# A graph network on one core: the 4-head attention layers carry segment maxima by VectorE transpositions, with fewer TensorE products and one GpSimd wait less

## The reference

```python
z = (x @ W).reshape(n, 4, 64)
el = jnp.sum(z * al, axis=-1)
er = jnp.sum(z * ar, axis=-1)
e = leaky_relu(el[src] + er[dst], 0.2)
e_max = segment_max(e, dst)
ex = jnp.exp(e - e_max[dst])
alpha = ex / segment_sum(ex, dst)[dst]
out = segment_sum(z[src] * alpha[:, :, None], dst) + x + b
out = elu(out)
```

## Time and profile before

| | |
|---|---|
| median of three timed runs | 3638.85 us |
| span of the profiled execution | 4213.3 us (the page gives no other time of it) |
| TensorE products / weight loads | 3393.7 us (81%) / 2079.6 us (49%) |
| VectorE | 1955.5 us (46%) |
| ScalarE | 1189.6 us (28%) |
| GpSimd | 1440.0 us (34%) |
| granted TensorE clock, mean | 0.787 of 2.4 GHz |
| 8-head layer | about 350 to 1260 us of the span |
| layers 1 to 4, by adjacency | about 1400 to 2560 us |
| 4-head layers | about 2580 to 3290 and 3370 to 4090 us |

### The profile page before, as it was taken

How to read it: one execution, slowest core, us unless ns; L and a number is a source line. 1 busy time by engine, 2 the same in 40 slices (tenths; PEclk the granted TensorE clock), 3 DMA queues, 4 the chain that set the end, 5 groups by cost and what they waited for, 6 DMA issues and landing times.

```text
span 4213.3 us, 58454 instructions
## 1 busy us (share of the span) xinstructions
PE 3393.7 (81%) x16476; PEld 2079.6 (49%) x16477; DVE 1955.5 (46%) x4442; ACT 1189.6 (28%) x3024; POOL 1440.0 (34%) x1472
## 2 busy tenths in 40 slices
PE   5887777777777999999999985777778757777766
PEld 3444554454554556456555553555555434555543
DVE  5986666666665200000024013444545734445556
ACT  2663333333331101001001004333333243333333
POOL 5003444444430302103003003655555255555530
PEclk8997887878786999999989997666666756566676
DMA  6235555555550231332311322333333133333320
GB/s 201 98 119 139 138 148 137 141 138 142 147 139 1 81 99 40 112 90 63 99 46 50 103 65 75 110 107 106 106 106 105 54 98 109 106 104 106 108 61 31
DMA packets 236395, 424.63 MB, mean 101 GB/s; under 512 B 51419, under 2 KB 152720, under 8 KB 235966
## 3 DMA queue, kind: packets, MB, share of 16 engines
q1 hardware_dynamic: 175549, 248.26, 20.3%
q0 software_dynamic: 60544, 173.03, 15.1%
HBM read 381.52 MB, written 39.62 MB: 100 GB/s over the span
## 4 chain that ended last, share of the span: by engine, by line
PE 54%; DVE 16%; issue 11%; another core or an unknown queue 10%; ACT 4%; DMA 2%; DVEq 2%; SPq 1%; ACTq 0%; POOL 0%; POOLq 0%
PE ps L734 20%; PE ps L807 9%; PE ps L612 3%; PE ps L577 3%; PE ps L968 3%; DVE norm L1438 2%; PE ps L948 2%; PE ps L918 2%; PE ps L910 2%; DVE rows L1569 1%; DVE inv L1675 1%; ACT norm L1117 1%; PE ps L801 1%; DVE spread L1428 1%
## 5 line engine op out<-in xcount | busy, mean ns | idle before, releaser
L2041 POOL DMA_INDIRECT rows<-table,src_idx x1248 | 1215.3, 974 | 1134.5 <-DVEq L1357 422.9
L734 PE MATMUL ps<-rows,rT 128*128 128x448 f16 (+1 forms) x3200 | 816.5, 342 | 16.8 <-DMA rows<-adjacency 16.8
L734 PE MATMUL ps<-rows,spread 128*128 128x448 f16 (+1 forms) x1600 | 546.5, 342 | 0.0
L734 PEld LDWEIGHTS ps<-rows,rT 128*128 128x128 bf16 x3200 | 311.9, 98 | 278.0 <-issue 25.0
L807 PE MATMUL ps<-rows,spread 128*128 128x260 f32 x832 | 364.2, 587 | 66.5 <-issue 59.4
L807 PE MATMUL ps<-rows,w_roots 128*128 128x260 f32 x832 | 359.0, 578 | 54.4 <-issue 52.2
L1454 DVE TENSOR_TENSOR rows<-ps,norm 128x896 f32<-128x896 f32 (+1 forms) x24 | 24.7, 1028 | 674.2 <-PE ps L734 674.2
L1995 POOL CAST rT<-rows 128x1024 bf16<-128x1024 f32 (+1 forms) x28 | 26.6, 950 | 868.9 <-ACT rows L1212 868.9
L577 PE MATMUL ps<-rT,spread 128*128 128x272 f32 x832 | 284.0, 471 | 36.8 <-DVE norm L1256 20.3
L612 PE MATMUL ps<-rows,rT 128*128 128x272 f32 x832 | 293.3, 511 | 2.5 <-DVE rows L1310 2.5
L807 PEld LDWEIGHTS ps<-rows,spread 128*128 128x128 f32 x832 | 225.7, 290 | 130.3 <-issue 84.6
(11 more groups left out here) (266 smaller groups left out, 5067.6 us busy)
## 6 DMA issues: line engine op xcount, KB each, us to landing
rows<-adjacency SPq DMA_DIRECT2D x140, 560.0 KB, 3.7
rT<-table SPq DMA_DIRECT2D x416, 136.0 KB
spread<-in_tiles SPq DMA_DIRECT2D x104, 256.0 KB
rows<-table,src_idx POOLq DMA_INDIRECT x1248
w_table<-in_tiles SPq DMA_DIRECT2D x52, 256.0 KB
adjacency<-rT SPq DMA_DIRECT2D x4, 2800.0 KB, 10.6
adjacency<-acc SPq DMA_DIRECT2D x3, 2800.0 KB, 11.7
table<-rows SPq DMA_DIRECT2D x12, 528.0 KB, 3.0
```

The lines of the kernel that those rows point to most:

```text
L734: ins = mm(chunk_ps[c % 2][:, f, 0:width], xp[k][:, t, f * P:(f + 1) * P], ring[c][q][:, i, :], start=t == 0 and k == 0, stop=t == ROWS - ...
L2041: pool.indirect_dma_start(src_rows(l, par)[:, k, :], None, tables[l][:, :], bass.IndirectOffsetOnAxis(ap=src_idx[:, g * T + k:g * T + k + ...
```

## The change

In the 4-head layers:
- `spread_scores` makes one product of 12 columns for each tile; the three parts stay apart in PSUM, and `edge_scores` first adds them by a VectorE reduction, ahead of its wait for the gathered rows.
- `edges` and `carries` of TensorE go. `carry` transposes the row ends of both scans (32x32) into `ends_row`, with the forward ends on partition 0 and the backward ends on partition 1, takes the maximum of the scans (before, the first operation of `maxima`), scans both ways over two partitions, copies the last value, and transposes two blocks back into a column (`carry_of`).
- `rescales` makes one product with `resc_by_f`, which ScalarE forms by a second exponential from the rescaling factor and a constant row that is 0 for the feature half of a head and very negative for the other.
- The two halves of the step's second sums are joined.
- SP loads the end penalties with one transfer instead of two; a group has three transfers.
- GpSimd no longer waits for `er_ready` at the fifth gather.
- VectorE's chained steps of one group are 8 instead of 5. The setup makes the new constants and no longer those of `perm`.

```diff
@@ gat_pe
-                    for part in range(PARTS):
-                        ins = mm(er_ps[:, k * H:(k + 1) * H], turned_hot[:, par, k, :],
-                                 near[:, par, k, part * H:(part + 1) * H], start=part == 0, stop=part == PARTS - 1)
+                    ins = mm(er_ps[:, k, :, :].rearrange("p k h -> p (k h)"), turned_hot[:, par, k, :], near[:, par, k, :],
+                             start=True, stop=True)
...
-                for f in range(FC):
-                    ins = mm(gat_resc_ps[:, f:f + 1], head_of[H][:, f, :], resc_h[par][0:H, :], start=True, stop=True)
-                ins.then_inc(resc_ready, 1)
+                mm(gat_resc_ps, head_any[:, :], resc_by_f[par][:, :], start=True, stop=True).then_inc(resc_ready, 1)
...
-                if n is not None:
-                    edges(n)
-                    if not is_last(n):
-                        spread_scores(n + 1, *next_group(j, h, 2))
-                sums(g, j, 1, range(4, 6))
-                if n is not None:
-                    carries(n)
-                sum_tiles(j % 2, j, range(6, 8)).then_inc(node_ready, 1)
+                if n is not None and not is_last(n):
+                    spread_scores(n + 1, *next_group(j, h, 2))
+                sums(g, j, 1, range(4, 8)).then_inc(node_ready, 1)
@@ gat_act, weights
+                nc.scalar.activation(resc_by_f[b % 2][:, :], other_f[:, :], ACT.Exp, bias=rescale[0:H, :])
@@ gat_dve
-                rows_landed(dve, l, b, h)
                 dve.wait_ge(er_ready, gl + n + 1)
-                ch.then(V.tensor_tensor(grid(al), er_ps.rearrange("p (t h) -> p t h", h=H), src_rows(l, b)[:, :, D:D + H], ALU.add))
+                ch.then(V.tensor_reduce(grid(al), er_ps.rearrange("p t k h -> p t h k"), AX.X, ALU.add))
+                rows_landed(dve, l, b, h)
+                ch.then(V.tensor_tensor(grid(al), grid(al), src_rows(l, b)[:, :, D:D + H], ALU.add))
...
+                dve.wait_ge(scans_ready, ag + n + 1)
+                ch.done(V.transpose(ends_row.rearrange("p h s -> p s h")[:, 1:T + 1, :], walks[0:TH, P - 1:P + 31]))
+                ch.then(V.tensor_tensor(gat_max_ps, fwd[0:TH, :], bwd[0:TH, :], ALU.max))
+                pr = gat_pen_row[:, j, :, :].rearrange("p h s -> p (h s)")
+                ends = ends_row[0:2, :, :].rearrange("p h s -> p (h s)")
+                V.tensor_tensor_scan(linked[0:2, 0:HL], pr, ends, -BIG, ALU.add, ALU.max)
+                ch.then(V.tensor_tensor_scan(linked[0:2, HL:2 * HL][:, ::-1], pr[:, ::-1], ends[:, ::-1], -BIG, ALU.add, ALU.max))
+                V.tensor_copy(ends_row[0:2, :, 0:1], linked[0:2, 0:HL].rearrange("p (h s) -> p h s", h=H)[:, :, T:T + 1])
+                into = linked[:, :].rearrange("p (j x) -> p j x", j=2)[:, :, 0:HL].rearrange("p j (h s) -> p j s h", h=H)
+                return ch.done(V.transpose(carry_of[:, :].rearrange("p (j t h) -> p j t h", j=2, h=H), into[:, :, 0:T, :]))
...
-                                                   carry_ps[0:TH, j:j + 1], gat_max_ps, ALU.add, ALU.max))
+                                                   carry_of[:, 33 * j:33 * j + 1], gat_max_ps, ALU.add, ALU.max))
@@ SP, seg
-                    for k in range(2):
-                        at = (2 * j + k) * H * SLOTS
-                        sp.dma_start(gat_pen_row[0:1, at:at + H * SLOTS].rearrange("o (h s) -> o h s", h=H)[:, :, 1 - k:SLOTS - k],
-                                     pen_ends[k:k + 1, bass.ds(g * T, T)].unsqueeze(1)
-                                     .broadcast_to([1, H, T])).then_inc(gat_seg_landed[j], 16)
+                    sp.dma_start(gat_pen_row[:, j, :, 1:T + 1],
+                                 pen_ends[:, bass.ds(g * T, T)].unsqueeze(1).broadcast_to([2, H, T])).then_inc(gat_seg_landed[j], 16)
@@ gpsimd
-                        if kind == "gat" and g > 0 and k == T // 2:
-                            wait_alone(pool, er_ready, NG * (l - 5) + g)
```

More of the change, by code:

```diff
@@ L53 @@
 SLOTS = T + 1
+LINKS = T + 2
 LAYERS = [("gat_edge", 8, D + 16), ("sum", 0, D), ("sum", 0, D), ("sum", 0, D), ("sum", 0, D),
@@ L73 @@
     STORES.append([v + _in_hbm * (b == _c % 2) for b, v in enumerate(STORES[-1])])
-SEG_LOADS = {0: 48, 5: 64, 6: 64}
+SEG_LOADS = {0: 48, 5: 48, 6: 48}
 SEGS = 4
@@ L181, in gnn_program @@
         left = sb("left", [P, 2, 4, 4])
-        gat_pen_row = sb("gat_pen_row", [1, SEGS * 2 * 4 * SLOTS])
+        gat_pen_row = sb("gat_pen_row", [2, SEGS, 4, LINKS])
         edge_pen_row = sb("edge_pen_row", [1, 4 * 8 * SLOTS])
-        perm = sb("perm", [33, 2, 4, SLOTS])
+        ends_row = sb("ends_row", [32, 4, LINKS])
+        linked = sb("linked", [32, 2 * (4 * LINKS + 2)])
+        carry_of = sb("carry_of", [32, 2 * 32])
         edge_perm = sb("edge_perm", [65, 2, 8, SLOTS])
@@ L238, in gnn_program @@
         resc_h = [sb(f"resc_h{p}", [8, 1]) for p in range(2)]
+        resc_by_f = [sb(f"resc_by_f{p}", [4, FC]) for p in range(2)]
+        head_any = sb("head_any", [4, P])
+        other_f = sb("other_f", [4, FC])
         part = [rows[:, i * FC * CW:(i + 1) * FC * CW].rearrange("p (f n) -> p f n", f=FC) for i in range(4)]
@@ L777, in turn_scores @@
                 nc.tensor.transpose(alT_ps[0:TH, :], al3[:, 0:TH], ident[:, :]).then_inc(alT_ready, 1)
[L779 to L790, removed]
             def turn_back(n):
@@ L867, in gat_pe @@
             turn_scores(0)
-            edges(0)
-            carries(0)
             turn_back(0)
@@ L1515, in gat_dve @@
             TH = T * H
-            HS = H * SLOTS
+            HL = H * LINKS
             ag, gl = NG * ATT.index(l), NG * (l - 5)
@@ L1541, in carry @@
             def carry(n, j):
[L1542 to L1548, removed]
@@ L1557, in maxima @@
+                V.tensor_copy(ends_row[0:2, :, 0:1], linked[0:2, 0:HL].rearrange("p (h s) -> p h s", h=H)[:, :, T:T + 1])
+                into = linked[:, :].rearrange("p (j x) -> p j x", j=2)[:, :, 0:HL].rearrange("p j (h s) -> p j s h", h=H)
+                return ch.done(V.transpose(carry_of[:, :].rearrange("p (j t h) -> p j t h", j=2, h=H), into[:, :, 0:T, :]))
+            def maxima(n, at, carried_at):
+                ch.wait(carried_at)
                 for j, into in ((0, gat_max_ps), (1, segmax[0:TH, :])):
@@ L1558, in maxima @@
                     ch.then(V.scalar_tensor_tensor(into, gat_pens[at][0:TH, P + 1 + j * P:2 * P + 1 + j * P],
-                                                   carry_ps[0:TH, j:j + 1], gat_max_ps, ALU.add, ALU.max))
+                                                   carry_of[:, 33 * j:33 * j + 1], gat_max_ps, ALU.add, ALU.max))
                 V.tensor_tensor(shifted[0:TH, :], alT_ps[0:TH, :], segmax[0:TH, :], ALU.subtract)
-                V.tensor_scalar(rescale[0:H, :], carry_ps[0:H, 0:1], segmax[0:H, 0:1], 0.0, ALU.subtract,
+                V.tensor_scalar(rescale[0:H, :], carry_of[0:H, 0:1], segmax[0:H, 0:1], 0.0, ALU.subtract,
@@ L1628, in step @@
                 if n is not None:
-                    carry(n, b)
+                    carried_at = carry(n, b)
                 rescale_node(g, j % 2)
                 if n is not None:
-                    maxima(n, b)
-            edge_row = perm[TH:TH + 1, :, :, :]
-            V.memset(fwd[TH:TH + 1, :], 1.0)
-            V.memset(bwd[TH:TH + 1, :], 1.0)
-            ch.then(V.memset(edge_row, 0.0))
-            ch.then(V.memset(edge_row[:, 0, :, 0:1], -BIG))
-            ch.then(V.memset(edge_row[:, 1, :, T:SLOTS], -BIG))
+                    maxima(n, b, carried_at)
+            V.memset(linked[:, :], 0.0)
+            ch.then(V.memset(ends_row[:, :, :], -BIG))
             turned_hots(0, 0, 0)
@@ L1642, in gat_dve @@
             scans(0, 0)
-            carry(0, 0)
-            maxima(0, 0)
+            maxima(0, 0, carry(0, 0))
             turned_hots(1, 1, 0)
@@ L2174, in _ @@
                 ins = V.tensor_tensor(ends_of_tile[:, j, :], seg_of_tile[:, :, x], seg_of_tile[:, :, y], ALU.not_equal)
-            V.memset(perm[:, :, :, :], 0.0)
+            V.tensor_tensor(head_any[:, :], head_of[4][:, 0, :], head_of[4][:, 1, :], ALU.add)
+            ch.then(V.tensor_tensor(other_f[:, :].unsqueeze(2), head_of[4][:, :, 0:1], head_of[4][:, :, P - 1:P], ALU.max))
             V.tensor_copy(ident16[:, :], ident[:, :])
-            V.memset(gat_pen_row[:, :], -BIG)
+            V.memset(gat_pen_row[:, :, :, :], -BIG)
             V.memset(edge_perm[:, :, :, :], 0.0)
@@ L2183, in _ @@
             for j in range(2):
-                ch.then(V.tensor_copy(perm[0:32, j, :, 1 - j:SLOTS - j], ident[0:32, 0:32].rearrange("p (t h) -> p h t", t=T)))
                 ch.then(V.tensor_copy(edge_perm[0:64, j, :, 1 - j:SLOTS - j], ident[0:64, 0:64].rearrange("p (t h) -> p h t", t=T)))
@@ L2208 @@
 EDGE_STEPS = 4 * 5
-GAT_STEPS = 4 * 5
+GAT_STEPS = 4 * 8
 INS = (["xT", "src_idx", "dst_idx", "base_row", "biases", "w_edge", "attrT"] + [f"w_table{s}" for s in range(NL)]
```

14 lines of the change are left out of this document (5 added, 9 removed).

## The result

| | before | after |
|---|---|---|
| median of 4 runs each, alternating | 3642.01 us (3636.05 to 3645.94) | 3619.24 us (3618.04 to 3626.04) |
| ratio of the times | 1 | 0.994, 95% interval 0.9928 to 0.9953 |
| recorded span, clock | 4213.3 us, 0.787 | 3616.5 us, 0.884 |

What follows compares the result with a forecast made beforehand. It took TensorE's round at the slow clock to bound the 4-head groups at 10.3 us, just above GpSimd's 10.0. Terms: -30 (groups) - 13 (layer starts) = -43 us, 3638.85 - 43 = 3596 us; range 3535 to 3650 us.

Steps and rivals of the forecast that it cites:

- I take 10.3 us for a group before: 4-head layers: estimated unrecorded time of one group before the change, between 10.1 and 10.9 us.
- two accounts, 10.1 and 10.9 us: Two ways to split the recording's 574.5 us excess between 8-head and 4-head layers, giving a 4-head group's unrecorded time.
- The tighter account: 8-head layer loses only VectorE's waits on TensorE, 260 us; 314 us left for 104 4-head groups, so 10.1 us each.
- the term of -30 us: 4-head loop: TensorE's round drops under GpSimd's 10.0 us, worth 0.3 us in each of some 100 groups.
- Rival 1: 4-head groups: GpSimd bounds already, removed products are hidden, only layer starts gain; 3616 to 3626 us, chance 0.22.
- The signs that the prediction named for the layers: Profile after: no 16.78 us GpSimd gap, burst of 8 products, no VectorE carry wait, gathers every 1.25 us.
- TensorE's round, 11.15 us at the slow clock: 4-head group: TensorE's summed pieces at 1.2 GHz take 11.15 us, and 9.7 us after the change.
- Sizes of the new operations: VectorE's reduction 0.25 us, transpositions 0.2 and 0.3; ScalarE's activation 0.19; one rescale product fewer saves TensorE 0.47.
- Layer starts, -13 us: Two 4-head layer starts: without GpSimd's fifth-gather wait the first step begins some 6.4 us sooner in each.
- Rival 4: 4-head groups: VectorE work stretches GpSimd's gathers by 0.06 x 8 = 0.5 us a group, floor 10.5; slower, 3668 us, chance 0.13.
- The records: 4-head layers: a smaller score-product burst shortens the recorded span more than the time, by 150 to 300 us.
- The queue rule: TensorE behind its densest burst: an internal trace-record queue holds back its producer and loses nothing; no size given.

Runs made afterwards that it cites:

- second recording: The kernel before, recorded once more without any edit: 3648.1 us, span 3646.3 us.
- the wait alone: The kernel before with only GpSimd's wait at the fifth gather taken out: 3625.39 us, ratio 0.9955.
- before with two edits only: The kernel before without GpSimd's fifth-gather wait and with the layer-start score copies written in memory order: 3606.31 us, ratio 0.9903, best time with the fewest edits.
- the kernel with copies on two engines: The kernel after, its four layer-start copies of turned destination scores in the old order, two on ScalarE and two on VectorE: 3608.37 us, ratio 0.9912.

## Where the prediction failed, and where it held

**The step that failed: "I take 10.3 us for a group before".** The prediction had two accounts, 10.1 and 10.9 us, and its own floor of 10.0 for GpSimd. The tighter account left 314 us of the excess to the 4-head layers, by the rule that the 8-head layer loses exactly its waits for TensorE. The second recording shows 5.1 x 52 = 265 us there, against the 260 of that account, and 10.05 us for the 4-head group. What the prediction holds against 10.1 is that GpSimd waits in 37 of 38 groups of the first recording. But those waits were themselves part of the excess that the account had just taken out, so they were counted twice. From 10.3 followed the term of -30 us, 0.3 in each of 100 groups. There is no such 0.3: GpSimd set the pace at 10.05 us already, and all edits but the wait give 3.6 us, which can't be told from nothing. Rival 1 (GpSimd bounds already, 3616 to 3626 us) was the case that came: 3619.24 us lies in it. That it also lies in the stated range of 3535 to 3650 us says little, since the range is 115 us wide.

**Signs that couldn't decide.** The signs that the prediction named for the layers came: the 16.78 us gap is gone, the burst is 8 products (312 in 39 groups), the wait at the carry is gone, and the gathers follow each other at 1.25 us. But rival 1 leads to the same rows after the change. Only the kernel before, recorded again or with less work on GpSimd, tells the two apart.

**TensorE's round, 11.15 us at the slow clock, 1.43 us less by the change.** Wrong in both numbers as a statement on the loop. With two gathers less, the loop of before runs at 8.8 to 9.05 us, and all edits together shorten it by 0.2 us. The sum was built from one group of a recording in which TensorE was held up. The pieces were summed as if one came behind the other on one path, which no experiment shows to be so.

**Sizes of the new operations.** Taken 0.25, 0.2 and 0.3 us; measured 0.237 for the reduction, 0.216 and 0.279 for the transpositions. The activation of 4x2 was put at 0.19 and takes 0.279. The rescale product costs 14.0 us in 40 groups, 0.35 each, where two products cost 23.5 us in 39 (0.60): 0.25 saved, not 0.47. None of it shows in the time, because VectorE then waits for gathered rows up to 3.7 us a group.

**Layer starts, -13 us.** Right in mechanism and close in size. The experiment with the wait alone measures 17.7 us, with an interval that holds 13, and its stream of gathers is 6.5 us shorter in one layer (530.6 against 537.1) and 7.1 in the other, where the prediction had 6.4 in each. "It is not a new stop; then it waits for the first free buffer, which comes 6.4 us sooner too": that wait is the one left, 7.10 us after the whole change. The prediction priced the difference and didn't see that the rest was a gap worth closing. By the spans of GpSimd's stream the whole change gives 6.1 + 8.0 = 14.1 us in the two layers. The rest of the 22.8 us isn't settled by them. The stretch between the two layers' gathers, which the change leaves alone, took between 100.2 and 105.8 us in the recordings, and the first gather of the first 4-head layer came between 2310.9 and 2321.1 us (the first recording left out). Differences of that size can't be placed.

**Rival 4 (gathers stretched by VectorE).** Not shown. The mean gather went from 0.951 to 0.957 us, a tenth of what the rival asked for, and even that can't be laid to the new VectorE work: before with two edits only, which has none of it, has 0.955 and 0.956 in the two layers, and the kernel with copies on two engines, which has all of it, 0.952 and 0.954. The Trainium skill, "SBUF — State Buffer", section "SBUF: two separate sides", has some VectorE operations lock a port pair against GpSimd; the traces agree as far as they go. Of the gathers above 1.05 us in the 4-head layers, 16 of 22 before (second recording) and 22 of 34 after overlap the making of the one-hot tiles (L1524, L1508), which only one gather in seven does. They are too few to weigh on the time.

**The records.** "The recorded span falls by 150 to 300 us more than the time": it fell by 574 us more, and for another reason. The 8-head layer, whose code the change leaves alone, lost its excess too. TensorE's idle time ahead of the sum products, which follow the burst, first recording (2700 to 3200 us) and second (2400 to 2800 us):

```profile
PE ps L807 <- issue: 50.1, 46, 2.4
PE ps L807 <- issue: 0.2, 1, 0.2
```

The second recording has the same bursts, 960 products at L771 in 400 us, and none of that idle time. So the burst alone does not bring it about. The queue rule that the prediction cited from the Trainium skill ("NOTIFIC — the notification-queue block", section "7.1 Overflow: three behaviours, one of which stalls the engine") is neither shown nor refuted by this; it stays a possible cause of the first recording only.

## What to carry to other kernels

When a recorded span is far above the timed runs, find the stretches that carry the excess, and then take the waits of these stretches as part of it: judge the bound by what remains, here GpSimd's 0.95 + 0.30 us eight times a group against the 10.1 of the tighter account. A quick test of a bound is to take a quarter of its work away and see whether the loop shrinks, and how far. Where one engine's stream is the bound, look for its gaps alone, at the starts of loops and layers; here a gap of 16.5 us at the start of each of two layers held nearly all that the best version won (33 of 35.5 us), and a rewrite of the products in the loop gave nothing that shows.

## What the hardware showed that I had not expected

- One recording of an unchanged kernel was 567 us longer than the next (4213.3 and 3646.3 us), in the layers with gathers, while all timed runs of it lie between 3633.90 and 3648.10 us.
- A copy of 1248 numbers a partition from PSUM to bf16 takes 5.96 us when PSUM is read in a row and each number is written 96 bytes from the last, and 1.21 us when 12 are written side by side and PSUM is read in steps. The slow order costs the same on ScalarE and VectorE, alone (5.96 each) or side by side (6.09 and 6.05).
- Once in each turn of the hardware loop VectorE stands still for 4.1 us, released by nothing that the profile shows. With GpSimd out of the way, that group takes about 12.4 us instead of 8.1 to 8.9. With eight gathers a group GpSimd's stream shows nothing of it; that the four buffers even it out is my reading and wasn't tested.
